# Joined expert stage of an eight-block kernel: time mixing on VectorE, products placed later, first statistics ahead of the last add

## The reference

```
# L1_attn: time mixing (RWKV); x is one normalised sequence, last_x the same sequence one token earlier
k = Wk @ (x * mix_k + last_x * (1 - mix_k))     # and v, r in the same way
num = alpha + exp(time_first + k) * v           # alpha, beta: sums over earlier tokens,
den = beta  + exp(time_first + k)               # decayed by ew = exp(-exp(time_decay)) per token
rwkv = sigmoid(r) * num / den
out = Wo @ rwkv

# L2_ffn, its second half: mixture of 8 experts, the best 2 of each token
gate = top-2 of softmax(t @ router)
hid  = silu(t @ w1[e]) * (t @ w3[e])
y    = x + sum over e of gate[:, e] * (hid @ w2[e])
```

## Time and profile before

| What | Value |
|---|---|
| three timed runs | 3718.06, 3730.5 and 3747.28 us, median 3730.5 |
| profiled execution | 3722.94 us, span 3721.2, mean granted clock of PE 0.883 of full speed |
| busy over the span | PE 2961.2 us (80%), DVE 2359.2 (63%), ACT 1568.3 (42%), POOL 770.9 (21%) |
| the three joined stages | start at 888, 1799 and 2718 us of the span, some 126 to 129 us each |
| the time mixing that runs once | 183 to 217 us |

### The profile page before, as it was taken

How to read it: one execution, slowest core, us unless ns; L and a number is a source line. 1 busy time by engine, 2 the same in 40 slices (tenths; PEclk the granted TensorE clock), 3 DMA queues, 4 the chain that set the end, 5 groups by cost and what they waited for, 6 DMA issues and landing times. The chain is left out here.

```text
span 3721.2 us, 89913 instructions
## 1 busy us (share of the span) xinstructions
PE 2961.2 (80%) x35888; PEld 2004.3 (54%) x35888; DVE 2359.2 (63%) x6687; ACT 1568.3 (42%) x3160; POOL 770.9 (21%) x823
## 2 busy tenths in 40 slices
PE   3778888689877788869986878876998687798996
PEld 2535556556554455556654445655655354475654
DVE  7574755665776466466667745646567775565457
ACT  4144535444434353535342544453434354444432
POOL 4121312221113221221111312131111122212101
PEclk8688999699988899969998889987999798999998
DMA  1011000000001100000000110000010101000000
GB/s 41 1 36 34 22 7 3 1 3 23 13 1 49 31 19 8 3 1 3 27 10 7 46 34 13 8 2 1 4 31 5 32 21 39 7 3 3 19 18 7
DMA packets 64209, 59.21 MB, mean 16 GB/s; under 512 B 16371, under 2 KB 53156, under 8 KB 63782
## 3 DMA queue, kind: packets, MB, share of 16 engines
q1 hardware_dynamic: 62550, 52.72, 5.2%
q10 hardware_dynamic: 1232, 0.61, 0.1%
HBM read 35.76 MB, written 2.10 MB: 10 GB/s over the span
## 5 line engine op out<-in xcount | busy, mean ns | idle before, releaser
L1333 POOL TENSOR_TENSOR l1t_ss<-l1t_ss,neghalf 128x16 f32<-128x16 f32 x48 | 182.3, 3798 | 338.9 <-DVE l1t_ss L1367 338.9
L256 ACT ACT_TABLE_LOAD x64 | 82.1, 1283 | 304.6 <-PEq L1677 106.5
L2260 ACT ACTIVATE l2r_P<-l2r_bank_score 128x512 f32<-128x512 f32 x240 | 130.2, 595 | 135.7 <-PE l2r_bank_score L1982 135.7
L2260 ACT ACTIVATE l2a_P<-l2a_bank_score 128x512 f32<-128x512 f32 x240 | 130.2, 595 | 129.0 <-PE l2a_bank_score L1982 129.0
L1544 PE MATMUL l1t_ring<-l1f_qkv,x_normT 128*128 128x512 f32 x288 | 171.5, 728 | 11.4 <-ACT x_normT L1238 11.4
L191 POOL TENSOR_TENSOR ln_y_rstd<-ln_var_eps,neghalf 128x4 f32<-128x4 f32 x52 | 52.8, 1015 | 541.4 <-DVE ln_var_eps L212 505.7
L2152 DVE CUSTOM_DVE_ANT_0 l2r_masked<-l2r_bank_ring,l2r_neg_wide 128x512 bf16<-128x512 f32 (+1 forms) x192 | 111.5, 622 | 57.6 <-PE l2r_bank_ring L1951 57.3
L2152 DVE CUSTOM_DVE_ANT_0 l2a_masked<-l2a_bank_ring,l2a_neg_wide 128x512 bf16<-128x512 f32 (+1 forms) x192 | 111.7, 621 | 53.5 <-PE l2a_bank_ring L1951 52.5
L1951 PE MATMUL l2r_bank_ring<-l2r_k_head,l2r_q_head 32*128 32x128 f32 x1824 | 131.2, 285 | 14.9 <-DVE l2r_m L2152 7.4
L1982 PE MATMUL l2r_bank_score<-l2r_q_head,l2r_k_head 32*128 32x128 f32 x1920 | 140.4, 283 | 2.0 <-DMA l2r_q_head<-l2r_shiftT 0.9
L1982 PE MATMUL l2a_bank_score<-l2a_q_head,l2a_k_head 32*128 32x128 f32 x1920 | 139.5, 282 | 1.8 <-DMA l2a_q_head<-l2a_shiftT 0.8
(11 more groups left out here) (1197 smaller groups left out, 8416.0 us busy)
## 6 DMA issues: line engine op xcount, KB each, us to landing
l1t_v_low<-l1t_v SPq DMA_DIRECT2D x84, 130.0 KB, 2.3
l2x_w<-in_L_ffn_w SPq DMA_DIRECT2D x72, 128.0 KB, 2.3
l1f_qkv<-in_L_ffn_wqkv SPq DMA_DIRECT2D x6, 768.0 KB, 4.4
l1t_v_low_last<-l1t_v_last SPq DMA_DIRECT2D x28, 130.0 KB, 2.3
l1f_tables<-in_l_tables SPq DMA_DIRECT2D x6, 512.0 KB, 5.7
l2e_w_last<-in_L_ffn_w SPq DMA_DIRECT2D x24, 128.0 KB, 2.2
x_in<-in_L_attn_hidden_states SPq DMA_DIRECT2D x8, 256.0 KB, 3.1
out<-x_res SPq DMA_DIRECT2D x8, 256.0 KB, 2.6
```

Source lines behind the costliest of these rows:

```text
L256: act.activation(b.warm[:, column:column + 1], b.neghalf[:, 0:1], func)
L1333: pool.tensor_tensor(ss[:, n % 2], ss[:, n % 2], b.neghalf[:, 0:2 * H8], ALU.pow).then_inc(s["rn_ready"], 1)
L2260: act.activation(self.P[:, use % self.P_RING].rearrange("k h q -> k (h q)"), self.score_bank(h, g)[:, :], ACT.Exp, scale=self.scale).then_ ...
```

## The change

1. **Mixing on VectorE.** The folded weights go. For each sequence VectorE computes the difference `dx = x - last_x` and then `mixed[c] = dx * mix_c + last_x` for k, v and r (four operations on 128x512); each projection is then one product, which waits for its own mixed input. This is done in `l1_attn` and in the joined stage; preparation loses six operations on 128x128.
2. **Order in `l1_attn`.** The mixes of both sequences come ahead of the scans, and the denominator is computed in place, after the numerator's product.
3. **Order in the joined stage.** `SIDE` gets other counts. The front's projections, results, normalisation and exponentials move to later steps on PE and ScalarE. On VectorE `mix` is added, the reciprocal is split off `denominator`, and it comes after the mixes of the second sequence.
4. **Statistics.** The statistics of the experts' sum of sequence 0 come ahead of the last add, those of sequence 1 after what is left of the front. On POOL the experts' roots are interleaved with the front's.

How the front's VectorE operations fall into the steps, as counted from the generator and `SIDE` (before | after, with 0 and 1 for the sequence; M0 and M1 are the two multiplications):

| step | before: after M0; after M1; after the add | after the change |
|---|---|---|
| 3 | 1; 1; 3 quantise | 1; 1; 4 quantise |
| 4 | 1; 1; 3 quantise | 1; 1; 4 quantise |
| 8 | add rows 1; statistics 1; variance 1, negative mean 1 | add rows 1; statistics 1; variance 1, difference 0 and mix k0 |
| 9 | none; scan beta 0; den 0 | negative mean 1; mix r0; mix v0 |
| 10 | sum 0; reciprocal 0 first half; second half | scan beta 0; den 0; difference 1, mix k1, mix r1 |
| 11 | key times value 0; scan alpha 0; numerator 0 and result 0 | mix v1; sum 0; reciprocal 0 both halves |
| 12 | scan beta 1; den 1; sum 1, reciprocal 1 first half | key times value 0; scan alpha 0; numerator 0 and result 0 |
| 13 | reciprocal 1 second half; key times value 1; scan alpha 1 | scan beta 1; den 1; sum 1, reciprocal 1 first half |
| 14 | product 1; numerator 1; result 1, statistics 0 | reciprocal 1 second half; key times value 1; scan alpha 1, product 1, numerator 1 |
| 15 | variance 0; add rows 0; statistics and variance 1 | result 1; statistics 0; variance 0, add rows 0 |
| after the last add | add rows 1 | statistics and variance 1, add rows 1 |

The diff, cut to its core:

```diff
@@ l1_attn, vector @@
             pre_norm(dve, step, b, s)
+            for p in range(PAIR):
+                last_x = b.xT_pad[:, p, 3:3 + S]
+                dve.wait_ge(s["xT_ready"], p + 1)
+                step(dve.tensor_tensor(dx[:, p, :], b.xT[:, p, :], last_x, ALU.subtract))
+                step.settle()
+                for c, mix, ready in (("k", w["mk"], s["xk_ready"]), ("v", w["mv"], s["xv_ready"]), ("r", w["mr"], s["xr_ready"])):
+                    dve.scalar_tensor_tensor(mixed[c][:, p, :], dx[:, p, :], mix[:, 0:1], last_x,
+                                             ALU.mult, ALU.add).then_inc(ready, 1)
...
-                step(dve.tensor_tensor_scan(beta[:, p, 1:], ew, ek[:, p, :], 0.0, ALU.mult, ALU.add))
                 dve.wait_ge(s["v_ready"], p + 1)
                 step(dve.tensor_tensor(ekv[:, p, :], ek[:, p, :], v_ps[p][:, :], ALU.mult))
+                step(dve.tensor_tensor_scan(beta[:, p, 1:], ew, ek[:, p, :], 0.0, ALU.mult, ALU.add))
                 step.settle()
                 step(dve.tensor_tensor_scan(alpha[:, p, 1:], ew, ekv[:, p, :], 0.0, ALU.mult, ALU.add))
+                step.settle()
                 dve.wait_ge(s["exp_uk_ready"], p + 1)
-                step(dve.tensor_tensor(den[:, p, :], euk[:, p, :], beta[:, p, 0:S], ALU.add))
-                step.settle()
 
                 step(dve.tensor_tensor(ekv[:, p, :], euk[:, p, :], v_ps[p][:, :], ALU.mult))
+                step.settle()
+                step(dve.tensor_tensor(euk[:, p, :], euk[:, p, :], beta[:, p, 0:S], ALU.add))
+                step.settle()
+                step(dve.tensor_tensor(ekv[:, p, :], ekv[:, p, :], alpha[:, p, 0:S], ALU.add))
                 dve.wait_ge(s["exp_r_ready"], p + 1)
...
-SIDE = [(0, 0, 0), (1, 1, 3), (1, 1, 3), (1, 1, 3), (1, 1, 3), (1, 1, 3), (1, 1, 2), (1, 1, 1), (1, 1, 2),
-        (0, 1, 1), (1, 1, 1), (1, 1, 3), (1, 1, 2), (1, 1, 1), (1, 1, 2), (1, 1, 2)]
+SIDE = [(0, 0, 0), (1, 1, 3), (1, 1, 3), (1, 1, 4), (1, 1, 4), (1, 1, 3), (1, 1, 0), (1, 1, 1), (1, 1, 2),
+        (1, 1, 1), (1, 1, 3), (1, 1, 2), (1, 1, 3), (1, 1, 2), (1, 1, 3), (1, 1, 2)]
@@ joined stage, gpsimd @@
             rstd(s1, f.yrs, "post", 0)
+            pool.wait_ge(s["post_var"], 1)
+            pool.tensor_tensor(b.yrs[:, 0, :], b.ve[:, 0, :], b.neghalf[:, 0:NT], ALU.pow).then_inc(s["post_rstd"], 1)
             rstd(s1, f.yrs, "post", 1)
-            pow_rstd(pool, b, s, post=True)
+            pool.wait_ge(s["post_var"], 2)
+            pool.tensor_tensor(b.yrs[:, 1, :], b.ve[:, 1, :], b.neghalf[:, 0:NT], ALU.pow).then_inc(s["post_rstd"], 1)
...
@@ joined stage, vector @@
+            def mix(p):
+                last_x = f.xT_pad[:, p, 3:3 + S]
+                dve.wait_ge(s1["xT_ready"], p + 1)
+                step1(dve.tensor_tensor(dx[:, p, :], f.xT[:, p, :], last_x, ALU.subtract))
+                yield
+                step1.settle()
+                for c in "krv":
+                    dve.scalar_tensor_tensor(mixed[c][:, p, :], dx[:, p, :], w_att["m" + c][:, 0:1], last_x,
+                                             ALU.mult, ALU.add).then_inc(s1[f"x{c}_ready"], 1)
+                    yield
...
                 yield from pre_stats(s1, step1, 1)
+                later = mix(0)
+                next(later)
+                next(later)
+                yield
                 negative_mean(s1, 1)
                 yield
+                yield from later
                 yield from denominator(0)
+                yield from mix(1)
+                yield from reciprocal(0)
                 yield from numerator(0)
                 yield from denominator(1)
+                yield from reciprocal(1)
                 yield from numerator(1)
...
+            rows = [b.yn[:, p].rearrange("t j d -> t (j d)") for p in range(PAIR)]
+            post_stats(dve, step, b, s, rows, 0)
             add(len(experts) - 1)
             for _ in side:
                 pass
-
-            post_norm(dve, step, b, s, [b.yn[:, p].rearrange("t j d -> t (j d)") for p in range(PAIR)])
+            post_stats(dve, step, b, s, rows, 1)
+            for p in range(PAIR):
+                post_apply(dve, step, b, s, rows, p)
@@ joined stage, tensor @@
             def project(c, p, free, ready):
                 pe.wait_ge(free, p + 1)
-                pe.matmul(turned[p][:, :], w_att["now_" + c][:], f.xT[:, p, :], start=True, stop=False)
-                pe.matmul(turned[p][:, :], w_att["w" + c][:], f.xT_pad[:, p, 3:3 + S], start=False,
-                          stop=True).then_inc(ready, 1)
+                pe.wait_ge(s1[f"x{c}_ready"], p + 1)
+                pe.matmul(turned[p][:, :], w_att["w" + c][:], mixed[c][:, p, :], start=True, stop=True).then_inc(ready, 1)
...
+                if n == 9:
+                    project("k", 0, s1["xT_ready"], s1["k_ready"])
                 if n == 10:
+                    turn(s1, s1["xn_act"], f.xn, 1)
+                if n == 11:
                     project("v", 0, s1["exp_r_ready"], s1["v_ready"])
-                    turn(s1, s1["xn_act"], f.xn, 1)
-                if n == 12:
+                    project("k", 1, s1["xT_ready"], s1["k_ready"])
+                if n == 13:
                     result(0)
-                if n == 15:
-                    result(1)
                 up(n, 1)
...
-                if n == 8:
-                    project("k", 0, s1["xT_ready"], s1["k_ready"])
-                if n == 9:
+                if n == 10:
                     project("r", 0, s1["exp_uk_ready"], s1["r_ready"])
-                if n == 10:
-                    project("k", 1, s1["xT_ready"], s1["k_ready"])
-                if n == 11:
+                if n == 12:
                     project("r", 1, s1["exp_uk_ready"], s1["r_ready"])
-                if n == 12:
+                if n == 13:
                     project("v", 1, s1["exp_r_ready"], s1["v_ready"])
+                if n == 15:
+                    result(1)
                 if n:
                     down(n - 1)
@@ prepare, vector @@
             dve.wait_ge(s["loaded"], 16 * len(b.moves))
-            for c in "kvr":
-                step(dve.tensor_scalar(l1a["now_" + c][:], l1a["w" + c][:], l1a["m" + c][:, 0:1], None, ALU.mult))
-            step.settle()
-            for c in "kvr":
-                step(dve.tensor_tensor(l1a["w" + c][:], l1a["w" + c][:], l1a["now_" + c][:], ALU.subtract))
```

More of the change, by code:

```diff
@@ L1041, in bank @@
             return [ctx.enter_context(nc.psum_tensor(f"l1a_{name}{p}" + b.tag, [128, 512], F32)) for p in range(PAIR)]
-        den = sb("den", [128, PAIR, S])
+        dx = sb("dx", [128, PAIR, S])
+        mixed = {c: sb("x" + c, [128, PAIR, S]) for c in "kvr"}
         ek, euk, er = sb("exp_k", [128, PAIR, S]), sb("exp_uk", [128, PAIR, S]), sb("exp_r", [128, PAIR, S])
@@ L1106, in _ @@
             for p in range(PAIR):
-                pe.wait_ge(s["xT_ready"], p + 1)
-                for c, ps, ready in (("k", k_ps, s["k_ready"]), ("v", v_ps, s["v_ready"]), ("r", r_ps, s["r_ready"])):
-                    pe.matmul(ps[p][:, :], w["now_" + c][:], b.xT[:, p, :], start=True, stop=False)
-                    pe.matmul(ps[p][:, :], w["w" + c][:], b.xT_pad[:, p, 3:3 + S], start=False, stop=True).then_inc(ready, 1)
+                for c, wc, ps, got, ready in (("k", w["wk"], k_ps, s["xk_ready"], s["k_ready"]),
+                                              ("v", w["wv"], v_ps, s["xv_ready"], s["v_ready"]),
+                                              ("r", w["wr"], r_ps, s["xr_ready"], s["r_ready"])):
+                    pe.wait_ge(got, p + 1)
+                    pe.matmul(ps[p][:, :], wc[:], mixed[c][:, p, :], start=True, stop=True).then_inc(ready, 1)
             for p in range(PAIR):
@@ L2751, in l2_ffn_experts_and_front @@
         ekv, rw = sb("exp_k_v", [128, PAIR, S]), sb("rwkv", [128, PAIR, S])
+        dx, mixed = sb("dx", [128, PAIR, S]), {c: sb("x" + c, [128, PAIR, S]) for c in "kvr"}
         alpha, beta = sb("alpha", [128, PAIR, S + 1]), sb("beta", [128, PAIR, S + 1])
@@ L2808, in _ @@
             rstd(s1, f.yrs, "post", 0)
+            pool.wait_ge(s["post_var"], 1)
+            pool.tensor_tensor(b.yrs[:, 0, :], b.ve[:, 0, :], b.neghalf[:, 0:NT], ALU.pow).then_inc(s["post_rstd"], 1)
             rstd(s1, f.yrs, "post", 1)
-            pow_rstd(pool, b, s, post=True)
+            pool.wait_ge(s["post_var"], 2)
+            pool.tensor_tensor(b.yrs[:, 1, :], b.ve[:, 1, :], b.neghalf[:, 0:NT], ALU.pow).then_inc(s["post_rstd"], 1)
+            own = Steps(pool, s["offset_ready"])
+            pool.wait_ge(s["post_rstd"], PAIR)
+            own(pool.tensor_tensor(b.gain[:], b.ymv[:, :, :, 0], b.yrs[:], ALU.mult))
+            own.settle()
+            own(pool.tensor_tensor(b.offset[:], b.offset[:], b.gain[:], ALU.add))
+            own.settle()
             add_offset(s1)
@@ L2906, in denominator, with reciprocal @@
                 yield
+            def reciprocal(p):
```

(2 more changed lines are left out.)

22 lines of the change are left out of this document (10 added, 12 removed).

## The result

The changed kernel takes 3755.1 us (median of 20 runs, 3742.2 to 3767.9) against 3726.5 for the kernel before: +28.6 us, a ratio of 1.0081 [1.0068, 1.0095]. The forecast was +16.8 us, 3743, with 3764 as its upper end: the direction and the range held, the size did not. The profiled execution took 3767.9 us, the longest of the 20; 45 us lie between the two profiled executions, so stages are compared by their own length, and wholes by medians.

What follows compares the result with a forecast made beforehand. PE was taken as the bound, with VectorE's queue deciding at its three stops. Three joined stages at 1.7 + 4.4, less 3.1, plus 1.6 gave +16.8 us on a middle of 3726.7: 3743 us, range 3712 to 3764.

Steps and rivals of the forecast that it cites:

- The waits of PE: Joined stage: PE waits 1.7 and 0.3 us ahead of the key products, 3.3 and 3.7 ahead of the results.
- Rival 1: PE stays the bound to the end; joined stages gain 4.8 us each, about 3714 us; chance 0.22.
- rival 4: VectorE reaches everything later by the same amount, joined stages keep their length: +1.6 us, 3728; chance 0.04.
- A joined stage at full clock: Each joined stage becomes 1.7 us longer before any slow clock is counted.
- The tail: Joined stage from result 1 to the next stage: 17.8 us, 16.0 before, with three uncovered waits for POOL's root.
- The clock: PE at half clock behind the two long result waits costs +4.4 us per joined stage.
- Rival 2: The clock holds: the waits come in joined stages without slow stretches behind them, +6.7 us, 3733; chance 0.18.
- rival 3: Clock stays down from the wait ahead of result 0 to the joined stage's end: +46.6 us, 3773; chance 0.06.
- the -3.1 of the sum: Slow-clock cost that the second joined stage already pays, taken off because its causes are replaced: 3.1 us.
- The single stage: Time-mixing stage that runs once: mixes add 2.4 us and VectorE's waits between chained operations 0.5, about 2.9 longer.
- The preparation: Preparation loses six operations that nothing hides: -1.3 us.
- 3 x (1.7 + 4.4) - 3.1 + 1.6 = +16.8 us: Whole kernel: three joined stages, less slow-clock cost already paid, plus single stage and preparation together.

Runs made afterwards that it cites:

- Experiment 2: The changed kernel with both reciprocals back in their old place, ahead of the expert adds: 3728.7 us, 1.0007 of the kernel before.
- experiment 4: The changed kernel's order with the folded weights of before, so no mixing on VectorE and two products per projection: 3740.1 us, 1.0035 of the kernel before.
- Experiment 1: The changed kernel with 12 and 14 extra PE products in the two waits ahead of the results in each joined stage: 3750.7 us, 1.0055 of the kernel before.
- experiment 8: The kernel before with three unused semaphores added in the single time-mixing stage, cleared by SP ahead of the loop: 3740.1 us, 1.0037 of the kernel before.
- experiment 9: The changed kernel with one semaphore in place of three for the single stage's six mixes: 3742.9 us, 1.0040 of the kernel before.
- experiment 6: The kernel before with only the experts' first post statistics moved ahead of the last expert add: 3719.7 us, 0.9980 of the kernel before.
- experiment 12: The changed kernel with reciprocals and key mixes ahead of expert adds, last aggregate ahead of the last add, single stage folded as before: 3708.1 us, 0.9939 of the kernel before.

## Why the prediction was right, and where its size was wrong

- **The waits of PE** were right: 1.7, 0.3, 3.3 and 3.7 us forecast, 1.92, 0.43, 3.17 and 3.66 measured. The queue of VectorE could be added up from rows of the kernel before. Experiment 2 shows that the place of the two reciprocals makes the growth of the result waits, and experiment 4 that the order does so without any mixing; what the later products add is not shown by itself. Rival 1 falls, and rival 4 too, since the joined stages did not keep their length.
- **A joined stage at full clock**: +1.7 forecast. Experiment 1, with the clock held, gives (402.1 - 394.2) / 3 = +2.6 us, where 394.2 is three times the 131.4 of an undisturbed stage before. The tail has its share of the 0.9 more: 15.1 us from the add of the last expert but one to the next stage (1018.16 to 1033.27), forecast 17.8 - 3.0 = 14.8, with the two uncovered roots in their places; the third did not show as an idle.
- **The clock**: +4.4 per stage forecast, 2.3 to 3.8 measured by experiment 1. The forecast took its 4.4 us at half clock from another stage; here the stretches are 3.4 us, except for 6.8 in the first stage of the one profile. Rival 2 falls with it, and rival 3 too: the clock came back within 6.8 us. (Both rivals leave out the -3.1 of the sum; with it they would be 3730 and 3770.) Joined stages together: 15.2 forecast, 15.6 in this profile and 14.5 on the mean of three. That this is so close is partly luck: the part at full clock was too small by 0.9 us a stage, the clock too large by 0.6 or more.
- **The single stage**: 2.9 forecast, 3.5 measured. A mix takes 0.75 us at a spacing of 0.66 to 0.67, not 0.60 (190.06, 190.73): six of them make up 0.4 of the 0.6. By the Trainium skill, VectorE: DVE Perf Modes, section "The DRAIN you can't avoid", a semaphore between chained operations (copies, there) costs nothing extra; in this stage chained products start 0.72 to 0.73 us apart (197.88, 198.60, 199.33) and unchained ones 0.60 to 0.61 (199.33, 199.94), so the trace disagrees again. The preparation: -1.3 forecast, -1.0 measured.
- **The step that failed** is the sum, "3 x (1.7 + 4.4) - 3.1 + 1.6 = +16.8 us": it has no term for SP. The part on the single stage counts VectorE's operations and not the three semaphores that the mixes bring, which SP clears ahead of the loop. That term measured 12 to 13 us (+12.3 in experiment 8, -13.5 in experiment 9), and 10.7 by the stages of all profiles. 18.1 + 10.7 to 13.5 is 29 to 32, for 28.6 measured. The range held because it reached 21 us above the forecast, not because it allowed for this.

Two things stay open: what SP does in the 0.32 us, and the 8 us of experiment 6. For the first the records of SP's instructions give a hint. In each of the 42 turns of the fourteen profiles there is one long step of 0.82 to 0.87 us from one instruction to the next: behind the four transfers in the kernel before, three instructions earlier with the three clears, where it falls among the transfers, and one earlier with one. And 0.6 to 1.0 us after each of them an 8 KB packet moves on the DMA queue that the profiles' pages list as "q14 instruction". That points to the reading of further code at a fixed place of SP's list, but no run tests it.

## What to carry to other kernels

When work moves between engines, place the operations on the path first: here the joined stages lost some 14 us or gained 10, with the mixing and without it, by where two reciprocals stood in VectorE's queue. Count every instruction that a change issues on every queue, the clearing of semaphores too, and look at the short waits of untouched stages: one that grew by 0.3 us came with some 12. And compare the new order with the old amount of work before crediting either.

## What the runs showed of the hardware

- Three instructions more on SP ahead of a loop made a group of four transfers inside it 0.32 us longer in each turn (2.46, not 2.14); with one more it was 2.11.
- A wait of PE of 0.59 in place of 0.27 us went with an earlier fall of the granted clock to 0.50: the slow stretch at the end of the stage was 17.1 or 20.5 us in 19 of 21 turns, against 13.7 in all 21, and the two stages together took 3.6 us more in a turn.
- The length of a wait alone does not tell whether the clock falls: behind the same wait of 2.04 us, with the same products of PE after it, it fell in all three stages of experiment 2 (a product of the up pass takes 1.80 us) and held in all three of experiment 12 (1.02 us); behind 2.31 us it held in all three of experiment 4.
